# A diffusion block with windowed attention and 64 routed experts: batch 6's routing steps, the sends of rows, the expert accumulators and the last sums rearranged

## Chip, core and metric

The kernel runs on one core of one Trainium2 chip. The metric is the device time of one execution in microseconds. Of the kernel before three runs were made: 907.73, 908.15 and 908.41 us, median 908.15.

## What is computed

Input x is 8 batches of 512 tokens with 256 features, all fp32. In short:

```
mod = silu(c) @ wmod                     # 6 rows of 256 per batch: sa, ca, ga, sb, cb, gb
h = layernorm(x) * (1 + ca) + sa
x = x + ga * attention(h)                # 16 heads of 16, keys within 64 tokens, out projection
h = layernorm(x) * (1 + cb) + sb
scores = sigmoid(h @ gate_w.T)           # 64 experts in 8 groups
# best 4 groups by the sum of their two best (scores + bias), best 8 experts in them
# weights = scores of these, divided by their sum, times 2.5
# each expert takes its first 256 tokens (in token order), at most
y = (silu(buf @ w_gate[e]) * (buf @ w_up[e])) @ w_down[e]   # 256 -> 128 -> 256, per expert
x = x + gb * (sum over a token's experts of weight * y)
```

## The kernel before

It is written engine by engine, each with an instruction stream of its own and semaphores between them; nothing is scheduled by a compiler. There are three stages.

**Attention, with routing behind it.** The loop `batches` goes over the 8 batches. One batch has 20 slots (`SLOTS`: 4 groups of 4 heads, 5 key tiles each; slot = 5g + u). In each slot TensorE computes transposed scores for two pairs of heads (`scoresT`), ScalarE takes their exponentials (`exps`, semaphore `exp`, two per slot) and TensorE multiplies them by the values (`values`, semaphore `pv`, two per slot, but issued in bunches: key tiles 0 to 2 of a group at u = 3, tiles 3 and 4 at the next group's u = 0). VectorE takes row maxima ahead (L1453). Hidden between these lie the steps of the next batch (projections; tables `AT`, `SECOND`) and those of the batch before: output projection, x1, second layer norm, router. When each of these comes is written out by hand in the tables `BEHIND_IT` (batches up to 4), `LAST_BUT_TWO` (batch 5) and `LAST_BUT_ONE` (batch 6), which give slots of the batch that follows. Batch 7 has no batch behind it, its steps (`late_...`) come in halves of 256 tokens when attention is over.

The steps of a batch b that matter here, in order: `c_stats` (VectorE), `c_rstd` (GpSimd, four tiny operations per half of the tokens, L723 to L729, the last makes `nmean`), `c_xhat` (ScalarE, normalises into the row buffer H, L918, waits for `nmean`), `c_norm` (VectorE, L1508), `c_h2T` and `c_lg` (TensorE; they wait for both halves), `c_ex` (ScalarE, L929), `c_route` in 12 parts (VectorE, L1638; part 9 makes the chosen-expert mask and running counts, part 11 writes the weights and the token number into H, L1708 and L1710), `e_cnt` (TensorE, counts of tokens ahead), `e_key` (VectorE; makes `dest`, the slot numbers, L1724). For batch 7, `late_route` and `late_key` do the same per half (L1555, L1613, L1629).

**Sends.** GpSimd then writes each token's row to its 8 experts' buffers in DRAM (`slots_d`) by indirect DMAs (`send`, L746), one per 128 tokens and choice: 32 per batch. In the loop they are spread over slots: `SENDS_OF[b]` says how many in which slot, counted from the start of the following batch (slot 18 to 19, then 20 and on in the batch after that). The first send of a slot waits for `exp` of the slot before, the others for `pv`. GpSimd works in program order, and within a slot `a_rstd`, `wrap` and `c_rstd` stand ahead of the sends. What doesn't fit, and batch 7's 32, is sent behind attention, with the two halves of `c_rstd` of batch 7 between (L811 to L820).

**Experts.** When all sends have landed, SP loads the 256 rows of an expert (`load_slots`, 12 buffers `xg`, up to 8 experts ahead; from 12 on it waits for the rows of expert e - 12 to be added, L636), TensorE turns them (L1382), multiplies (L1394), ScalarE and VectorE make silu times up, TensorE multiplies by w_down (L1404), ScalarE scales with the token's weight (`scale_y`, L1018, 6 buffers `ys`), and GpSimd adds the rows to the tokens' sums in DRAM by two indirect DMAs per expert (`scatter`, L832; L827 writes without adding for the first expert of an accumulator). There are three accumulators `acc_d`; `ACC[e]` says which expert uses which, and a scatter waits until the last expert on the same accumulator has landed. Expert weights have 36 buffers and are loaded up to 36 experts ahead.

**Last sums.** SP loads the third accumulator into `f2` (`load_f2`, 512 KB per batch in four DMAs) and the gate row into `fg` (1 MB) behind the expert loop's other loads; then, when all rows are added, the other two accumulators of each batch into `fa` (L662). VectorE makes three sums per batch of 128x1024 (L1861, L1863, L1865: first plus second accumulator, plus the third, times the gate; the residual x1 is in accumulator 0 already and divided by the gate), and SP stores each (L666).

```
            def send_some(bt, rows, now, slot):
                for n, i in enumerate(rows):
                    if n == 0:
                        after(pool, "exp", now, 2 * slot)
                    else:
                        after(pool, "pv", now, 2 * slot)
                    send(bt, i)
```

## Time and profile before

| | |
|---|---|
| Runs | 907.73, 908.15, 908.41 us |
| The profiled execution | 907.57 us, span in the profile 905.8 us |
| TensorE busy | 681.8 us (75%) |
| GpSimd busy | 509.8 us (56%) |
| VectorE busy | 478.9 us (53%) |
| ScalarE busy | 394.4 us (44%) |
| Mean DMA rate | 211 GB/s, 191.47 MB |

The profiled execution's own time lies 1.8 us over its span (what is around the program) and 0.6 us under the median. In the timeline, attention runs to about 525 us, the sends behind it to 613, the experts to 868, the last sums to the end. Engines are called PE (TensorE), DVE (VectorE), ACT (ScalarE), POOL (GpSimd) and SP (the queue of most DMAs) in the rows. L with a number is a line of the kernel before. A busy share is a mean over stages with different limits, so the stages are read one by one. In a timeline the bracket at the end of a row is the idle time of the engine ahead of it and what ended it; "issue" there is time in which the engine waited for nothing that the profile shows.

### The profile page before, as it was taken

The page shows a single profiled execution, that of the slowest core. Times are in us where ns is not written, and L with a number is a line of the kernel's source. Part 1 is how long each engine was busy: PE and PEld are TensorE (multiplying, and loading weights), DVE is VectorE, ACT ScalarE, POOL GpSimd, SP SyncE. Part 2 cuts the span into 40 slices and gives each one's busy share as a digit, 9 for nine tenths or more (in the row PEclk, how much of TensorE's full clock was granted, in tenths as well). Part 3 has the DMA queues.
Part 4 walks back from the last instruction along what each step waited for, and adds up shares of the span by engine and source line. Part 5 has one row for each costly group of instructions (what it writes and reads, how often), then busy time and mean ns, then how long its engine had stood idle before and what let it go on. Part 6 is the DMA issues. An engine that isn't in the chain of part 4 may idle for free.

```text
span 905.8 us, 15461 instructions
## 1 busy us (share of the span) xinstructions
PE 681.8 (75%) x4760; PEld 466.9 (52%) x4787; DVE 478.9 (53%) x1964; ACT 394.4 (44%) x876; POOL 509.8 (56%) x519
## 2 busy tenths in 40 slices
PE   5679899999999999999797942006999888888000
PEld 3335556556566565565455522005888777676000
DVE  3065559869698697786787736201222222222048
ACT  2336566657566566665644511002444333334000
POOL 4000002057577476575767767772788888888810
PEclk9869999999999999999989975557999999999555
DMA  8684896748757577373536794107999998898997
GB/s 325 164 339 164 276 354 211 245 139 271 266 172 259 175 257 254 117 237 123 191 120 182 210 292 120 28 4 224 274 288 266 266 175 160 162 159 160 204 307 318
DMA packets 168334, 191.47 MB, mean 211 GB/s; under 512 B 22137, under 2 KB 150677, under 8 KB 168252
## 3 DMA queue, kind: packets, MB, share of 16 engines
q1 hardware_dynamic: 132220, 134.15, 46.6%
q0 software_dynamic: 30336, 38.03, 20.1%
q10 hardware_dynamic: 5696, 18.30, 5.3%
q8 instruction: 39, 0.64, 0.3%
q14 instruction: 43, 0.35, 0.1%
HBM read 100.64 MB, written 110.67 MB: 233 GB/s over the span
## 4 chain that ended last, share of the span: by engine, by line
PE 47%; POOL 14%; DMA 11%; DVE 10%; issue 9%; ACT 6%; ACTq 1%; SPq 1%; POOLq 0%; DVEq 0%
POOL acc_d L832 8%; PE outT L1171 7%; DMA acc_d<-ys,xg 7%; POOL slots_d L746 5%; PE scoresT L1394 5%; PE scoresT L1151 4%; PE stageA L1092 4%; PE scores L1129 4%; PE scoresT L1155 4%; PE stageA L1110 3%; PE stageC L1212 3%; ACT PT L890 2%; DMA Qs<-MT 2%; DVE junk L1453 2%; PE turns L1181 2%
## 5 line engine op out<-in xcount | busy, mean ns | idle before, releaser
L746 POOL DMA_INDIRECT slots_d<-H,dest x256 | 260.8, 1019 | 155.2 <-issue 87.9
L832 POOL DMA_INDIRECT acc_d<-ys,xg x124 | 191.6, 1545 | 55.0 <-issue 29.2
L1453 DVE CUSTOM_DVE_ANT_0 junk<-scores,mask 128x256 bf16<-128x256 f32 (+1 forms) x512 | 170.9, 387 | 72.1 <-PE scores L1129 70.8
L890 ACT ACTIVATE PT<-scoresT 128x512 f32<-128x512 f32 (+1 forms) x320 | 150.5, 509 | 47.5 <-PE scoresT L1155 45.6
L1394 PE MATMUL scoresT<-xgT,wgu 128*128 128x256 f32 x512 | 125.5, 388 | 17.5 <-ACT xgT L1005 17.4
L1151 PE MATMUL scoresT<-mask,identb 128*128 128x512 bf16 (+1 forms) x320 | 110.3, 345 | 18.7 <-ACT PT L890 14.5
L1394 PEld LDWEIGHTS scoresT<-xgT,wgu 128*128 128x128 f32 x512 | 95.4, 192 | 40.8 <-ACT xgT L1005 27.9
L1155 PE MATMUL scoresT<-Qs,Ks 98*128 98x256 bf16 (+1 forms) x640 | 110.9, 255 | 0.0
L1129 PE MATMUL scores<-Ks,Qs 96*128 96x256 bf16 (+1 forms) x512 | 93.7, 266 | 4.0 <-DVE mrowmax L1453 1.8
L1155 PEld LDWEIGHTS scoresT<-Qs,Ks 98*128 98x128 bf16 x640 | 64.0, 100 | 38.2 <-issue 8.6
L1171 PE MATMUL outT<-PT,Va 128*32 128x256 f32 (+1 forms) x1280 | 80.4, 356 | 1.8
L1842 DVE COPY xgT<-stageA 128x256 f32<-128x256 f32 x32 | 13.6, 425 | 118.2 <-PE stageA L1382 118.2
L874 ACT ACTIVATE parts<-stageA,bqk 128x512 bf16<-128x512 f32 x78 | 53.6, 687 | 42.3 <-PE stageA L1092 37.3
L1382 PE MATMUL scores<-ident,xg 128*128 128x128 f32 x128 | 24.9, 277 | 47.2 <-DMA xg<-slots_d 47.2
L1842 DVE COPY xgT<-stageC 128x256 f32<-128x256 f32 x32 | 13.6, 425 | 75.6 <-PE stageC L1382 75.6
L1151 PEld LDWEIGHTS scoresT<-mask,identb 128*128 128x128 bf16 x320 | 31.8, 99 | 39.8 <-ACT PT L890 22.2
L1005 ACT ACTIVATE xgT<-scores 128x256 f32<-128x256 f32 x64 | 24.7, 386 | 62.5 <-PE scores L1382 62.5
L1129 PEld LDWEIGHTS scores<-Ks,Qs 96*128 96x128 bf16 x512 | 44.4, 99 | 13.1 <-DVE mrowmax L1453 7.0
L1092 PE MATMUL stageA<-hT,wqkv 128*128 128x512 f32 x104 | 50.2, 605 | 0.0
L1171 PEld LDWEIGHTS outT<-PT,Va 128*32 128x32 f32 (+1 forms) x1280 | 28.9, 109 | 40.9 <-issue 25.2
L1018 ACT ACTIVATE ys<-outT,xg 128x256 f32<-128x256 f32 x64 | 26.9, 471 | 52.4 <-DMA acc_d<-ys,xg 45.3
L1018 ACT ACTIVATE ys<-turns,xg 128x256 f32<-128x256 f32 x64 | 26.9, 471 | 50.8 <-DMA acc_d<-ys,xg 43.1
(260 smaller groups left out, 1059.9 us busy)
## 6 DMA issues: line engine op xcount, KB each, us to landing
xg<-slots_d SPq DMA_DIRECT2D x64, 324.0 KB, 4.0
slots_d<-blank ACTq DMA_DIRECT2D x26, 648.0 KB, 5.2
parts_d<-parts SPq DMA_DIRECT2D x32, 384.0 KB, 3.4
Qs<-parts_d SPq DMA_DIRECT2D x96, 128.0 KB
Ks<-parts_d SPq DMA_DIRECT2D x90, 128.0 KB
acc_d<-zero SPq DMA_DIRECT2D x32, 272.0 KB
wgu<-L_ffn_w_gate_dram SPq DMA_DIRECT2D x64, 128.0 KB, 3.6
wgu<-L_ffn_w_up_dram SPq DMA_DIRECT2D x64, 128.0 KB, 3.7
```

What stands on the lines that cost most here:

```text
L746: pool.indirect_dma_start(out=slots_d[:, :], in_=H2[bt.par][:, t, :], in_offset=None, out_offset=bass.IndirectOffsetOnAxis(ap=dest[bt.par] ...
L832: pool.indirect_dma_start(out=acc_d[ACC[e]][:, :], in_=ys[e % NY][:, h, :], in_offset=None, out_offset=bass.IndirectOffsetOnAxis(ap=xg[e % ...
L874: sc_.activation(parts[:, j, k, :], bank[:, :], ACT.Identity, scale=SCALE if f < 2 else 1.0, bias=bqk[:, f:f + 1]).then_inc(sems["part"], 1)
L890: sc_.activation(PT[m % NPT][:, :, 0:w], src, ACT.Exp).then_inc(sems["exp"], 1)
L1018: sc_.activation(ys[e % NY][:, h, :], yb[:, h * D:(h + 1) * D], ACT.Copy, scale=xg[e % NX][:, h, D + e:D + e + 1]).then_inc(mo["yc"], 1)
L1092: last = mm(bank[:, :], wqkv[:, k, f * P:(f + 1) * P], hT[:, k, BAND:BAND + S], start=(k == 0), stop=(k == C - 1))
L1129: last = mm(bS[n % 2][:, i * 2 * P + lo:i * 2 * P + hi], q[0:MROW, h, t * P:(t + 1) * P], kk[0:MROW, h, t * P + lo:t * P + hi], start=True ...
L1151: mm(bST[m % 2][:, 0:2 * (hi - lo)].rearrange("p (h q) -> p h q", h=2), identb[:], half.unsqueeze(1).to_broadcast([P, 2, hi - lo]), start= ...
L1155: last = mm(bST[m % 2][:, i * (hi - lo):(i + 1) * (hi - lo)], kk[0:KROWS, h, u * P:(u + 1) * P], q[0:KROWS, h, lo:hi], start=False, stop=T ...
L1171: last = mm(bO[32 * j:32 * j + 32, lo:hi], Va[bt.par][rows, tile_of(u), HQ * g + j, :], PT[m % NPT][rows, i, 0:hi - lo], start=(u == 0), s ...
L1394: last = mm(bST[par][:, a * CAP:(a + 1) * CAP], wgu[e % NW][:, a, k, :], xgT[par][:, k, :], start=(k == 0), stop=(k == C - 1))
L1453: ins = v.tensor_tensor_reduce(out=junk[:, i, lo:hi], in0=bS[n % 2][:, i * 2 * P + lo:i * 2 * P + hi], in1=mask[:, lo:hi], scale=1.0, scal ...
```

## The change

- For batch 6 (`LAST_BUT_ONE`) `c_rstd`'s second half, `c_xhat`, `c_norm` and the first `c_h2T` come a slot later; the routing parts come up to two slots earlier, the count at slot 17 instead of 19.
- Batch 5's rows are sent three per slot instead of two, batch 6's four in slots 18 and 19 instead of two, and behind attention 11 and 2 sends instead of 8 and 2 stand around the halves of `c_rstd`. In every batch the second and later sends of a slot wait for `exp` (this slot's first) instead of `pv`.
- The third accumulator is used up to expert 26 instead of 53. Its loads into `f2` (32 DMAs of 128 KB) and that of `fg` go into the expert loop of SP, one per expert from 27 on, each behind a wait for TensorE's output of that expert. For that half of `f2` lies below the expert buffers in SBUF and half above.
- ScalarE scales expert 0 right behind taking expert 1's rows.
- GpSimd makes the last sums of batches 1 and 4, with a semaphore of its own; VectorE those of the other six. SP stores in order of the batches as before.

```diff
--- before.py
+++ after.py
@@ -113,13 +113,13 @@
     x1_store=(11,),
     xs=(10,),
     stats2=(4, 5),
-    c_rstd=(5, 5),
-    xhat=(5, 6),
-    norm2=(6, 7),
-    h2T=(8, 10),
+    c_rstd=(5, 6),
+    xhat=(6, 7),
+    norm2=(7, 8),
+    h2T=(9, 10),
     lg=(11,),
-    route=(11, 12, 13, 13, 13, 14, 14, 15, 15, 16, 17, 18),
-    cnt=(19,),
+    route=(11, 12, 12, 13, 13, 13, 14, 14, 15, 15, 16, 16),
+    cnt=(17,),
     key=(17,),
 )
 
@@ -199,8 +199,8 @@
 SENDS = sends_from(22, (1, 2, 2, 2, 1, 2, 1, 2, 2, 1, 2, 2, 2, 1, 2, 1, 2, 2, 1, 1))
 SENDS_OF = [SENDS] * B
 SENDS_OF[B - 4] = sends_from(22, (2, 2, 2, 2, 2, 2, 2, 2, 2, 2, 2, 2, 2, 2, 2, 2))
-SENDS_OF[B - 3] = sends_from(18, (2, 2, 2, 2, 2, 2, 2, 2, 2, 2, 2, 2, 2, 2, 2, 2))
-SENDS_OF[B - 2] = sends_from(18, (2, 2, 28))
+SENDS_OF[B - 3] = sends_from(18, (3, 3, 3, 3, 3, 3, 3, 3, 3, 3, 2))
+SENDS_OF[B - 2] = sends_from(18, (4, 4, 24))
 SENDS_OF[B - 1] = {}
 
 
@@ -417,10 +417,12 @@
         end = ExitStack()
         sb = lambda name, shape, dt=F32: sbt(end, name, shape, dt)
         fg = sb("fg", [P, B, D])
-        sb("beyond_the_start", [P, 7656 - B * D])
+        f2 = [sb(f"f2_{i}", [P, T, D]) for i in range(B // 2)]
+        sb("beyond_the_start", [P, 7656 - B * D - B // 2 * T * D])
         NF = 8
-        f2 = [sb(f"f2_{i}", [P, T, D]) for i in range(B)]
         fa = [sb(f"fa{i}", [P, 2, T, D]) for i in range(NF)]
+        sb("beside_experts", [P, NW * 3 * D - NF * 2 * T * D + NX * 2 * HW + 2 * C * CAP + 4 * CAP + NY * 2 * D])
+        f2 += [sb(f"f2_{i}", [P, T, D]) for i in range(B // 2, B)]
         end.close()
         eng_moe = dict(
             w_ld=[sem(f"weights_loaded{i}") for i in range(NW)],
@@ -430,12 +432,14 @@
             sg=sem("silu_done"),
             hm=sem("hidden_done"), yp=sem("expert_out_made"), yc=sem("expert_out_scaled"),
             f2_ld=sem("third_sums_loaded"),
-            f_ld=[sem(f"sums_loaded{i}") for i in range(NF)], fsum=sem("last_sums"),
+            f_ld=[sem(f"sums_loaded{i}") for i in range(NF)], fsum=sem("last_sums"), psum=sem("last_sums_by_gpsimd"),
             f_st=sem("out_stored"),
         )
         mo = eng_moe
 
-        ACC = [e % 3 if e < 54 else e % 2 for e in range(E)]
+        THIRD_ENDS = 27
+        POOL_SUMS = (1, 4)
+        ACC = [e % 3 if e < THIRD_ENDS else e % 2 for e in range(E)]
         NCONST = 26
         NSET = 4
         BLANKS = 32
@@ -625,11 +629,10 @@
             load_c(last)
             rows = slots_d.rearrange("(h p e) c -> p h e c", h=2, p=P)
 
-            def load_f2(b):
-                rows_added(sp, max(e for e in range(E) if ACC[e] == 2) + b)
-                for t in range(T):
-                    sp.dma_start(f2[b][:, t, :], acc_d[2][b * S:(b + 1) * S, :].rearrange("(p t) d -> p t d", p=P)[:, t, :]
-                                 ).then_inc(mo["f2_ld"], 16)
+            def load_f2(b, t):
+                rows_added(sp, max(e for e in range(E) if ACC[e] == 2))
+                sp.dma_start(f2[b][:, t, :], acc_d[2][b * S:(b + 1) * S, :].rearrange("(p t) d -> p t d", p=P)[:, t, :]
+                             ).then_inc(mo["f2_ld"], 16)
 
             def load_slots(e):
                 if e >= NX:
@@ -650,10 +653,12 @@
                 if e + NW < E:
                     sp.wait_ge(mo["yp"], e + 1)
                     load_w(slice(e + NW, e + NW + 1), e)
-
-            for b in range(B):
-                load_f2(b)
-            sp.dma_start(fg[:], mod_d[:, 4, :].unsqueeze(0).to_broadcast([P, B, D])).then_inc(s_fg, 16)
+                if THIRD_ENDS <= e < THIRD_ENDS + B * T:
+                    sp.wait_ge(mo["yp"], e + 1)
+                    load_f2(*divmod(e - THIRD_ENDS, T))
+                if e == THIRD_ENDS + B * T:
+                    sp.wait_ge(mo["yp"], e + 1)
+                    sp.dma_start(fg[:], mod_d[:, 4, :].unsqueeze(0).to_broadcast([P, B, D])).then_inc(s_fg, 16)
             for e in range(E - NY, E):
                 rows_added(sp, e)
 
@@ -666,15 +671,10 @@
                 sp.dma_start(out[i].rearrange("o (p t) d -> p (o t) d", p=P), fa[n][:, 0]).then_inc(mo["f_st"], 16)
 
             for b in range(B):
-                if b >= NF:
-                    sp.wait_ge(mo["f_st"], 16 * (b - NF + 1))
-                load_f(slice(b, b + 1), b % NF)
-                if b >= NF - 1:
-                    sp.wait_ge(mo["fsum"], 3 * (b - NF + 2))
-                    store_f(slice(b - NF + 1, b - NF + 2), (b + 1) % NF)
-            for b in range(B - NF + 1, B):
-                sp.wait_ge(mo["fsum"], 3 * (b + 1))
-                store_f(slice(b, b + 1), b % NF)
+                load_f(slice(b, b + 1), b)
+            for b in range(B):
+                sp.wait_ge(mo["psum" if b in POOL_SUMS else "fsum"], 3 * sum((i in POOL_SUMS) == (b in POOL_SUMS) for i in range(b + 1)))
+                store_f(slice(b, b + 1), b)
             sp.wait_ge(mo["f_st"], 16 * B)
 
 
@@ -751,10 +751,7 @@
             def send_some(bt, rows, now, slot):
 
                 for n, i in enumerate(rows):
-                    if n == 0:
-                        after(pool, "exp", now, 2 * slot)
-                    else:
-                        after(pool, "pv", now, 2 * slot)
+                    after(pool, "exp", now, 2 * slot + min(n, 1))
                     send(bt, i)
 
             def body(prev, now, nxt):
@@ -808,13 +805,13 @@
                 for i in range(sum(n for s, n in SENDS_OF[bt.b].items() if s < 2 * SLOTS), T * K):
                     send(bt, i)
             sent_before = sum(n for s, n in SENDS_OF[B - 2].items() if s < SLOTS)
-            for i in range(sent_before, sent_before + 8):
+            for i in range(sent_before, sent_before + 11):
                 send(pre, i)
             c_rstd(last, 0)
-            for i in range(sent_before + 8, sent_before + 10):
+            for i in range(sent_before + 11, sent_before + 13):
                 send(pre, i)
             c_rstd(last, 1)
-            for i in range(sent_before + 10, T * K):
+            for i in range(sent_before + 13, T * K):
                 send(pre, i)
             for i in range(T * K):
                 send(last, i)
@@ -841,6 +838,18 @@
                 if same:
                     rows_added(pool, same[-1])
                 scatter(e)
+
+            pool.wait_ge(s_fg, 16)
+            pool.wait_ge(mo["f2_ld"], 16 * B * T)
+            for n, b in enumerate(POOL_SUMS):
+                pool.wait_ge(mo["f_ld"][b], 32)
+                a = fa[b]
+                gp.tensor_tensor(a[:, 0], a[:, 0], a[:, 1], ALU.add).then_inc(mo["psum"], 1)
+                pool.wait_ge(mo["psum"], 3 * n + 1)
+                gp.tensor_tensor(a[:, 0], a[:, 0], f2[b][:], ALU.add).then_inc(mo["psum"], 1)
+                pool.wait_ge(mo["psum"], 3 * n + 2)
+                gp.tensor_tensor(a[:, 0], a[:, 0], fg[:, b, :].unsqueeze(1).to_broadcast([P, T, D]), ALU.mult
+                                 ).then_inc(mo["psum"], 1)
 
 
         @block.scalar
@@ -1023,7 +1032,9 @@
                 silu(e)
                 if e < E - 1:
                     take_x(e + 1)
-                if e > 0:
+                if e == 0:
+                    scale_y(0)
+                if e > 1:
                     scale_y(e - 1)
             scale_y(E - 1)
 
@@ -1855,15 +1866,19 @@
 
             dve.wait_ge(s_fg, 16)
             dve.wait_ge(mo["f2_ld"], 16 * B * T)
+            n = 0
             for b in range(B):
-                a = fa[b % NF]
-                dve.wait_ge(mo["f_ld"][b % NF], 32 * (b // NF + 1))
+                if b in POOL_SUMS:
+                    continue
+                dve.wait_ge(mo["f_ld"][b], 32)
+                a = fa[b]
                 v.tensor_tensor(a[:, 0], a[:, 0], a[:, 1], ALU.add).then_inc(mo["fsum"], 1)
-                dve.wait_ge(mo["fsum"], 3 * b + 1)
+                dve.wait_ge(mo["fsum"], n + 1)
                 v.tensor_tensor(a[:, 0], a[:, 0], f2[b][:], ALU.add).then_inc(mo["fsum"], 1)
-                dve.wait_ge(mo["fsum"], 3 * b + 2)
+                dve.wait_ge(mo["fsum"], n + 2)
                 v.tensor_tensor(a[:, 0], a[:, 0], fg[:, b, :].unsqueeze(1).to_broadcast([P, T, D]), ALU.mult
                                 ).then_inc(mo["fsum"], 1)
+                n += 3
 
 
 _INS = ["L0_attn_x", "L0_attn_w_qkv", "L0_attn_b_qkv", "L0_attn_w_out", "L0_attn_b_out", "L0_ffn_gate_w",
```

## Rows read from the trace of the kernel before

**Rows 1.** GpSimd's timeline behind attention: start us, us, engine line op out<-in [idle before <-releaser].
```profile
525.70 0.97 POOL L746 DMA_INDIRECT slots_d<-H,dest  x1 [6.16 <-DVE H L1710]
...
541.13 0.22 POOL L723 TENSOR_SCALAR ve<-mv 128x2 f32<-128x2 f32 x1
...
570.99 1.69 POOL L746 DMA_INDIRECT slots_d<-H,dest  x1 [0.30 <-DVE dest L1629]
...
611.35 0.97 POOL L746 DMA_INDIRECT slots_d<-H,dest  x1 [0.31 <-issue]
```

**Rows 2.** GpSimd's timeline at the end of the experts.
```profile
848.88 1.54 POOL L832 DMA_INDIRECT acc_d<-ys,xg  x1 [0.57 <-DMA acc_d<-ys,xg]
...
857.02 1.54 POOL L832 DMA_INDIRECT acc_d<-ys,xg  x1 [1.04 <-DMA acc_d<-ys,xg]
...
862.56 1.54 POOL L832 DMA_INDIRECT acc_d<-ys,xg  x1 [0.30 <-issue]
```

**Rows 3.** VectorE's timeline in the tail, first and last of 24 sums.
```profile
873.41 1.23 DVE L1861 TENSOR_TENSOR fa<-fa 128x1024 f32<-128x1024 f32 x1 [35.16 <-DMA fa<-acc_d]
...
901.50 1.22 DVE L1865 TENSOR_TENSOR fa<-fa,fg 128x1024 f32<-128x1024 f32 x1
```

**Rows 4.** Stretch 885 to 890: stretch, us, PE, PEld, DVE, ACT, POOL busy, PEclk, DMA share, GB/s.
```profile
885.00:890.00 5.00, 0.00 (x0) 0.00 (x0) 4.90 (x5) 0.00 (x0) 0.00 (x0) 0.50 1.02 406
```

**Rows 5.** ScalarE's timeline in batch 7.
```profile
492.69 1.09 ACT L918 ACTIVATE H<-x,nmean,rs 128x256 f32<-128x256 f32 x2 [4.61 <-POOL nmean L729]
...
502.82 0.75 ACT L890 ACTIVATE PT<-scoresT 128x256 f32<-128x256 f32 x2
...
509.83 0.38 ACT L929 ACTIVATE ex<-stageC 128x256 f32<-128x256 f32 x1 [1.33 <-PE stageC L1230]
```

**Rows 6.** GpSimd's timeline in batches 6 and 7.
```profile
473.06 0.98 POOL L746 DMA_INDIRECT slots_d<-H,dest  x1 [0.30 <-ACT PT L890]
...
489.69 0.97 POOL L746 DMA_INDIRECT slots_d<-H,dest  x1 [0.30 <-issue]
...
490.73 0.45 POOL L723 TENSOR_SCALAR ve<-mv 128x2 f32<-128x2 f32 x1
...
492.38 0.20 POOL L729 TENSOR_TENSOR nmean<-nmean,rs 128x2 f32<-128x2 f32 x1
```

**Rows 7.** VectorE's timeline, batches 6 and 7.
```profile
468.23 0.18 DVE L1724 TENSOR_SCALAR dest<-near 128x32 uint32<-128x32 f32 x1
...
524.60 0.16 DVE L1710 COPY H<-token 128x4 int32<-128x4 int32 x1
...
560.97 0.17 DVE L1629 TENSOR_SCALAR dest<-near 128x16 uint32<-128x16 f32 x1
```

**Rows 8.** GpSimd's timeline at the start of the experts.
```profile
628.06 1.58 POOL L832 DMA_INDIRECT acc_d<-ys,xg  x1 [15.74 <-ACT ys L1018]
...
637.80 1.55 POOL L832 DMA_INDIRECT acc_d<-ys,xg  x1 [1.08 <-ACT ys L1018]
```

**Rows 9.** Scatter-adds issued from 728 to 750: issue to landing.
```profile
DMA to landing us min/median/max: 3.7/4.1/5.3
```

**Rows 10.** Stretch 740 to 760, columns as in rows 4.
```profile
740.00:760.00 20.00, 17.68 (x91) 14.25 (x89) 4.48 (x11) 7.53 (x21) 16.65 (x12) 1.00 0.92 160
```

**Rows 11.** Chain that ended last: start us, us, what.
```profile
862.56 5.71 DMA acc_d<-ys,xg
```

**Rows 12.** GpSimd's timeline in the setup.
```profile
2.26 0.56 POOL L698 TENSOR_SCALAR minus<-ident 128x128 bf16<-128x128 f32 x1
...
13.68 0.90 POOL L795 MEMSET Va<- 128x960 f32 x1
...
17.15 0.29 POOL L717 COPY hT<-hT 128x128 f32<-128x128 f32 x1
```

**Rows 13.** One sum of VectorE and one send of GpSimd, timelines of both.
```profile
505.72 1.22 DVE L1514 TENSOR_TENSOR x<-x,mr 128x1024 f32<-128x1024 f32 x1
...
506.10 1.69 POOL L746 DMA_INDIRECT slots_d<-H,dest  x1 [0.30 <-issue]
```

## The prediction

> **What bounds the kernel now.** The page's costliest groups come first: GpSimd's indirect sends of rows (L746) and its scatter-adds (L832) head them. The timelines by engine then show three stretches that GpSimd or VectorE sets. (a) After attention GpSimd issues the 64 sends of batches 6 and 7 without a pause, the first at 525.70, the last at 611.35, one each 1.28 us; the first had waited 6.16 us for VectorE's routing of batch 6 [rows 1]. The experts can't begin before the last has landed. (b) In the experts GpSimd issues two scatters per expert, 1.85 us apart, so 3.69 us per expert [rows 2]. TensorE, faster, waits. (c) In the last 37 us VectorE makes 24 sums back to back, 873.41 to 902.72, 29.3 us, three per batch of 3.66 [rows 3], while the DMAs run at 410 GB/s at full share [rows 4].
>
> The attention stretch before (a) counts as far as it sets when batch 6 is routed. Batch 7's attention has one large stall: ScalarE stands 4.61 us at the normalised rows of batch 6 until 492.69, released by GpSimd's `nmean`, whose c_rstd began at 490.73 right behind a send [rows 5, 6]. So c_rstd was late because of GpSimd's queue: 14 sends of batch 5, 473.06 to 489.69, each at 1.28 with no wait between [rows 6].
>
> **Part 1: three sends per slot, weaker waits.** Under two per slot GpSimd issues 7x2 = 14 sends of batch 5 ahead of c_rstd(6, first half), from slot 18 to slot 4. With three it issues 21. The new waits (`exp` for `pv`) take away GpSimd's idle time before 470, and batch 4's sends are done a few us sooner; but batch 5's still wait for its `dest`, made at 468.23 [rows 7]. From `H` at 524.60+0.16 to the first send at 525.70 passed 0.94 [rows 1, 7], so the first of batch 5 goes at about 469.3. 21x1.28 = 26.9 puts c_rstd's first half at 496.2 instead of 490.73: **5.5 us later**. Three more sends (3.84) and c_rstd's own 1.85 (490.73 to 492.58 [rows 6]) put the second half at 502.1 to 503.9. In other bodies c_rstd waits for VectorE or for nothing long, and I cost the new waits there at nothing: TensorE covers them.
>
> **Part 2: rows a slot further.** Shifting `c_rstd`, `xhat`, `norm2` by a slot lets ScalarE do slot 6's exponentials at about 491 ahead of the wait. Then it waits for `nmean` until 498.1; slot 7's exponentials; then it waits again, until 503.9, for the second half; slot 8's at 505 to 506. TensorE, two score banks deep, stands with it. Before, slot 9's exponentials ran at 502.82 and `ex` at 509.83 [rows 5], 7.0 us later; now slot 9 is at 506.6, so `ex` comes at 513.6 to 514.4. **+4.2 us.** Bounds: 0 (the stop only moves, and later slots take it up) and +6 (`h2T` of slot 9 takes TensorE some 1 us, and more of such small delays).
>
> **Part 3: routing two parts per slot, the count at slot 17.** From `ex` on VectorE runs without an idle time worth naming to `H` at 524.60 [rows 7], so moving its parts to earlier slots brings nothing: it works them off at its own pace. The count isn't the last wait either (`key` starts when VectorE is free). What changes: `norm_o` (0.7 us) now stands behind the histogram instead of ahead of it, and TensorE stands some 3 us at slot 17 for it; that delays batch 7's own end, which has 10 us of slack (below). Zero. So the first send of batch 6 goes at 525.70+4.2.
>
> **Part 4: behind attention.** 64 sends stay 64: slots 18 and 19 hold 8 instead of 4, then 11, 2 and the rest. c_rstd of batch 7 comes behind 19 sends instead of 12, so 4.2+7x1.28 = 13.2 us later than 541.13 [rows 1]. Batch 7's first `dest` follows: 560.97 [rows 7] goes to 574.2, and its first send, 570.99 before [rows 1], is wanted at 575.2. It just arrives; its second half has some 10 us. Zero here, but there is no slack left, and up to 1 us could show. Sum of parts 1 to 4: **+4.2**.
>
> **Part 5: first scale_y earlier.** Expert 0's scatters began at 628.06 [rows 8]. ScalarE can now scale it right behind `take_x(1)`, some 2.2 us earlier. But GpSimd waits again at expert 3, whose first scatter goes at 637.80, released by ScalarE, which was released by TensorE [rows 8]. That doesn't move. Zero.
>
> **Part 6: third accumulator ends at expert 27; f2 and fg loaded between experts.** In 27 to 53 an expert waits for the rows of the last but one, not the last but two. A scatter lands 4.1 us (median) after its issue there, 5.3 at most [rows 9]; the next on the same accumulator starts 3x1.85 = 5.54 after it, and GpSimd starts about 0.3 after a landing. So up to 5.24 costs nothing. The SP queue now adds a 128 KB load per expert behind the 324 KB of slots, where the DMAs are 0.92 busy in 740 to 760 [rows 10]. From 848 on, with such loads in bursts, two waits came, of 0.57 and 1.04 where 0.30 is usual [rows 2]: 1.0 us in some 8 experts. At that rate 33 experts cost 4.1; without any effect 0. I take 2: only the slower half of landings crosses 5.24, and a wait gives the next expert room. Against it: those two waits go (-1.0), and the last scatter, 862.56, no longer lands beside the 1 MB of fg; it took 5.7 us [rows 11] and will take 4.7 (-1.0). SP's first f2 load waits for expert 26's rows, so the slots of experts 36 on come 3 experts (11 us) later; 12 slot buffers and TensorE's lead over GpSimd cover it. Uncovered it would be 4 us of landing, once. Sum **0**, bounds -2 and +2.5.
>
> **Part 7: two of eight batches summed by GpSimd.** VectorE keeps 18 sums: 6x3.66 = 22.0 us. GpSimd gets 6 of 128x1024 with two operands in SBUF. No row has such a one. Below: it sets 960 columns in 0.90 [rows 12], so 0.96. Above: a scaled copy of 128 columns takes 0.56 [rows 12] against 0.20 for an operation on two columns [rows 6], so 1024 take 3.1. Between: its plain copy of 128 columns takes 0.29 [rows 12], 0.7 to 1 ns per column over its start, and with two operands to read twice that, **2.1 us**, which I take. 6x2.1 = 12.6.
>
> Do they run side by side? The rows say no, in one direction: a GpSimd send issued during a VectorE sum of two SBUF operands ends 0.84 us behind that sum. The sum 505.72+1.22 = 506.94, the send 506.10+1.69 = 507.79 [rows 13]; the same at 570.99 [rows 1] against 570.62+1.22. A free send takes 0.97. So GpSimd can't read while VectorE sums, and what one does adds to the other: 22.0+12.6 = 34.6 against 29.3, **+5.3 us** (bounds by the price: 27.8, -1.5; 40.6, +11.3). If they did run beside each other, VectorE would end at 897.5, held by the loads (8.4 MB at 0.41 are in at about 891.7), and the 12.6 MB of the stretch would end it near 901.5: **-4.3**.
>
> The Trainium skill, SBUF — State Buffer, "Who interferes with whom", says more than the row: a VectorE instruction with two SBUF inputs and a GpSimd instruction that reads SBUF exclude each other, whichever comes first. By it a GpSimd sum also stops VectorE's; the sum stays +5.3. The skill's GPSIMD Engine Reference, "3.1 Elementwise", gives 4497 ns for a GpSimd sum of 2048 fp32 columns, so by its figure some 2.25 us for 1024, and the tail's sum would be 22.0+13.5, +6.2. No row of this profile shows either.
>
> **Sum.** 4.2+0+0+5.3 = +9.5 on the profiled execution's 907.57 (span 905.8) is 917.1. The median of the runs is 0.58 above that execution: **917.7**.
>
> **The rivals.**
> Side by side: GpSimd's and VectorE's sums overlap after all (for it: only GpSimd was seen to wait, and its port time may be a small part of its instruction). Tail -4.3, the rest +4.2: 908.0, in a band of 904 to 911. It ends faster than before as soon as parts 1 to 6 cost less than 2.4 us. 0.24.
> Side by side, and the stall doesn't reach the routing (0 for parts 1 to 4): 903.9. This is the one on the other side: the place is the tail, the price 4.3, and it decides when the last batch's stop stays under 2.4 us. For it speaks that TensorE has slack at slots 12 to 19; against it that `ex` hangs on the second c_rstd by a chain with no slack. 0.12.
> Turns are taken in the tail, but the stall doesn't reach: 913.5. 0.16.
> My forecast, both: 917.7, own range 913.5 to 922. 0.48.
>
> **Numbers.** A measurement tells 0.2% (1.8 us) from nothing here. Faster: 0.12, and half of the first rival, 0.12: 0.24. Same: 0.12. Slower: the rest, 0.64. The range takes in the side-by-side cases and most of the upper bound: 903.5 to 922.
>
> **What would show it.** Right: ScalarE waiting on `nmean` twice in batch 7, some 6 and 4 us; batch 6's c_rstd at 496; the first send of batch 6 near 530, 64 without a pause behind it; sums in the tail stretched or spaced by 2 us, ending near 909 plus the shift. Wrong: c_rstd(6) at or before 491; `ex` before 511; VectorE's 18 sums at 1.22 with no gap beside GpSimd's; scatters spaced over 1.9 us on average (part 6 too low).

## The result, and where the time went

The changed kernel takes **922.35 us** (median of 4 runs, 917.35 to 924.2) where the one before, in the same session, takes 908.28 us (907.73 to 909.94): ratio **1.0155**, 95% interval 1.0126 to 1.0183. Forecast were 917.7 us and a range to 922.0; the direction is right, the size 4.65 us short, and the result lies 0.35 us above the range. The profiled execution took 924.2 us (span 922.4 us) against 907.57 us (905.8 us), 16.6 us more. It is read at six points, each the same instruction in both traces:

| point | before | after | later by | gained since the last |
|---|---|---|---|---|
| exponentials of slot 5, batch 7 | 485.85 | 487.72 | 1.87 | 1.87 |
| `ex` of batch 7 | 509.83 | 516.07 | 6.24 | 4.37 |
| last send | 611.35 | 617.68 | 6.33 | 0.09 |
| first scatter-add of expert 3 | 637.80 | 646.31 | 8.51 | 2.18 |
| first last sum on VectorE | 873.41 | 885.02 | 11.61 | 3.10 |
| end of VectorE's last sum | 902.72 | 919.39 | 16.67 | 5.06 |

The rows that answer to those of before. ScalarE's timeline of the changed kernel, batch 7 (as rows 5):

```profile
499.46 1.09 ACT L927 ACTIVATE H<-x,nmean,rs 128x256 f32<-128x256 f32 x2 [5.85 <-POOL nmean L729]
...
505.21 1.09 ACT L927 ACTIVATE H<-x,nmean,rs 128x256 f32<-128x256 f32 x2 [3.54 <-POOL nmean L729]
...
516.07 0.39 ACT L938 ACTIVATE ex<-stageC 128x256 f32<-128x256 f32 x1 [1.33 <-PE stageC L1241]
```

The one wait of 4.61 us for `nmean` has become two, 5.85 and 3.54 us. GpSimd's timeline of the changed kernel (as rows 6, 1, 8 and 2, then the last sums, which no row of before has):

```profile
470.79 0.97 POOL L746 DMA_INDIRECT slots_d<-H,dest  x1 [1.06 <-ACT PT L899]
...
496.68 0.97 POOL L746 DMA_INDIRECT slots_d<-H,dest  x1 [0.30 <-issue]
...
497.72 0.23 POOL L723 TENSOR_SCALAR ve<-mv 128x2 f32<-128x2 f32 x1
...
503.47 0.23 POOL L723 TENSOR_SCALAR ve<-mv 128x2 f32<-128x2 f32 x1
...
532.16 0.97 POOL L746 DMA_INDIRECT slots_d<-H,dest  x1 [15.68 <-DVE dest L1735]
...
617.68 0.98 POOL L746 DMA_INDIRECT slots_d<-H,dest  x1 [0.30 <-issue]
...
633.49 1.58 POOL L829 DMA_INDIRECT acc_d<-ys,xg  x1 [14.84 <-ACT ys L1027]
...
639.77 1.01 POOL L824 DMA_INDIRECT acc_d<-ys,xg  x1 [2.81 <-ACT ys L1027]
...
646.31 1.55 POOL L829 DMA_INDIRECT acc_d<-ys,xg  x1 [1.26 <-ACT ys L1027]
...
848.20 1.55 POOL L829 DMA_INDIRECT acc_d<-ys,xg  x1 [2.92 <-DMA acc_d<-ys,xg]
...
876.03 1.55 POOL L829 DMA_INDIRECT acc_d<-ys,xg  x1 [0.30 <-issue]
...
888.34 2.62 POOL L847 TENSOR_TENSOR fa<-fa 128x1024 f32<-128x1024 f32 x1 [10.75 <-DMA fa<-acc_d]
891.04 3.20 POOL L849 TENSOR_TENSOR fa<-fa,f 128x1024 f32<-128x1024 f32 x1
...
904.16 3.20 POOL L851 TENSOR_TENSOR fa<-fa,fg 128x1024 f32<-128x1024 f32 x1
```

c_rstd of batch 6 starts at 497.72 instead of 490.73, right behind a send. GpSimd had waited longer ahead of its sends of batch 6 (15.68 us for `dest`, since batch 5's were out earlier), so the time won there went into a wait. The 64 sends then took 85.5 us from the first to the last start, as before (85.65): no gap opened. In the experts GpSimd now waits for landed rows. All scatter-adds issued from 728 to 750, issue to landing, changed kernel (as rows 9):

```profile
DMA to landing us min/median/max: 3.9/5.3/6.7
```

That is a short window of 12. Over the whole stretch in question, the 54 scatter-adds of experts 27 to 53, first the kernel before, then the changed one:

```profile
DMA to landing us min/median/max: 3.7/4.0/5.3
...
DMA to landing us min/median/max: 3.8/4.8/6.7
```

The stretch from the first scatter-add of expert 27 to that of expert 53, in the kernel before:

```profile
726.57:822.71 96.14, 84.38 (x420) 68.00 (x418) 21.71 (x53) 36.93 (x106) 80.30 (x52) 1.00 0.90 162
```

Stretches of the changed kernel (columns as rows 4; the second is that of experts 27 to 53):

```profile
620.00:640.00 20.00, 15.06 (x54) 11.88 (x55) 2.69 (x7) 5.43 (x12) 3.40 (x3) 0.66 0.78 232
...
735.39:834.42 99.03, 83.39 (x420) 68.30 (x418) 21.33 (x53) 36.55 (x103) 80.64 (x52) 1.00 0.96 197
905.00:910.00 5.00, 0.00 (x0) 0.00 (x0) 4.93 (x4) 0.00 (x0) 2.36 (x1) 0.50 0.37 150
```

Over experts 27 to 53 the DMAs move 197 GB/s at a share of 0.96 where they moved 162 at 0.90, a scatter-add lands in 4.8 us (median) instead of 4.0, and the stretch takes 99.03 us instead of 96.13. In the 20 us from 740 to 760 alone the rate is 241 against 160 [rows 10]; the first loads of `f2`, issued in a bunch from 737.64 on, fall there. From 905 on the DMAs are at 0.37: in the tail they wait for the engines, where before they ran at 406 GB/s [rows 4]. VectorE's timeline in the tail of the changed kernel (as rows 3):

```profile
885.02 1.23 DVE L1875 TENSOR_TENSOR fa<-fa 128x1024 f32<-128x1024 f32 x1 [31.48 <-DMA fa<-acc_d]
...
890.75 1.28 DVE L1875 TENSOR_TENSOR fa<-fa 128x1024 f32<-128x1024 f32 x1 [1.99 <-DMA fa<-acc_d]
892.08 3.25 DVE L1877 TENSOR_TENSOR fa<-fa,f 128x1024 f32<-128x1024 f32 x1
...
905.19 3.24 DVE L1879 TENSOR_TENSOR fa<-fa,fg 128x1024 f32<-128x1024 f32 x1
...
918.17 1.22 DVE L1879 TENSOR_TENSOR fa<-fa,fg 128x1024 f32<-128x1024 f32 x1
```

Five of VectorE's sums take 3.24 to 3.35 us instead of 1.22, each beside a sum of GpSimd of 3.20; when GpSimd is done they are back at 1.22.

### The profile page after: what moved, and what is told of

The parts are those of the page before. It is cut to its first block, busy times and chain, and to the rows that moved or that the text cites. A ratio compares the mean times of both kernels' runs of the same rounds, so it can differ in the third digit from the quotient of the medians.

```text
span 922.4 us, 15494 instructions
## 1 busy us (share of the span) xinstructions
PE 689.8 (75%) x4760; PEld 471.5 (51%) x4787; DVE 482.7 (52%) x1958; ACT 396.0 (43%) x876; POOL 529.1 (57%) x525
## 4 chain that ended last, share of the span: by engine, by line
PE 46%; POOL 17%; issue 11%; DVE 11%; DMA 7%; ACT 5%; SPq 1%; ACTq 1%; DVEq 0%; POOLq 0%
POOL acc_d L829 10%; PE outT L1182 7%; POOL slots_d L746 5%; PE stageA L1103 5%; PE scoresT L1162 4%; PE scoresT L1405 4%; PE scores L1140 4%; PE scoresT L1166 4%; DMA acc_d<-ys,xg 3%; PE stageA L1121 3%; PE stageC L1223 3%; ACT PT L899 2%; DVE junk L1464 2%; PE turns L1192 1%; PE stageC L1241 1%
## 5 line engine op out<-in xcount | busy, mean ns | idle before, releaser
L1405 PE MATMUL scoresT<-xgT,wgu 128*128 128x256 f32 x512 | 127.4, 393 | 23.3 <-ACT xgT L1014 23.3
L1405 PEld LDWEIGHTS scoresT<-xgT,wgu 128*128 128x128 f32 x512 | 97.3, 195 | 46.3 <-ACT xgT L1014 32.3
L1182 PE MATMUL outT<-PT,Va 128*32 128x256 f32 (+1 forms) x1280 | 82.5, 364 | 1.8
```

Of the source, the lines that this page charges most:

```text
L1182: last = mm(bO[32 * j:32 * j + 32, lo:hi], Va[bt.par][rows, tile_of(u), HQ * g + j, :], PT[m % NPT][rows, i, 0:hi - lo], start=(u == 0), s ...
L1405: last = mm(bST[par][:, a * CAP:(a + 1) * CAP], wgu[e % NW][:, a, k, :], xgT[par][:, k, :], start=(k == 0), stop=(k == C - 1))
```

## The experiments

All but four ran in sessions where the kernel before takes 907.4 to 908.2 us. The other four (e9 to e12) ran in one where it takes 985.75; what that session shows is told at the end. Each ratio is against runs of before in the same session. Where an edit is a part of the change, its hunks are those shown in the change. No kernel leaves any part of the computation out.

**e1_sums: part 7 alone.**

```diff
+        POOL_SUMS = (1, 4)
...
+            for n, b in enumerate(POOL_SUMS):
...
```

VectorE's loop goes over the other six batches.

> The kernel before, with part 7 alone: GpSimd makes the last sums of batches 1 and 4. Theory (they take turns at the SBUF read port): as forecast +5.3 us, VectorE's sums stretched from 1.22 to about 3.25 us while GpSimd has work (the 2.0 over are what GpSimd holds the port). Rival (side by side): -4.3 us, VectorE's 18 sums at 1.22. Second rival: in the changed kernel the stretching comes from something else of the change (the place of f2 in SBUF); then this run is faster or equal.

Measured 913.28 us (911.89 to 917.26), ratio 1.0072 (1.0044 to 1.0099). VectorE's timeline in its tail, first sum and one beside GpSimd:

```profile
874.01 1.22 DVE L1872 TENSOR_TENSOR fa<-fa 128x1024 f32<-128x1024 f32 x1 [35.44 <-DMA fa<-acc_d]
...
884.34 3.25 DVE L1876 TENSOR_TENSOR fa<-fa,fg 128x1024 f32<-128x1024 f32 x1
...
907.16 1.22 DVE L1876 TENSOR_TENSOR fa<-fa,fg 128x1024 f32<-128x1024 f32 x1
```

From first start to last end 34.37 us (908.38-874.01), the same as in the whole change, against 29.3: the price is this part's own and needs none of the others. Both side-by-side rivals fall.

**e2_attn: parts 1 to 4 alone.** Edit: the slot table, both lists of sends, the waits in `send_some`, and 11, 2 for 8, 2 behind attention.

> The kernel before, with parts 1 to 4 alone (slots of batch 6, two routing parts per slot, three sends per slot, new waits, 4+4+11+2 sends). Theory (c_rstd of batch 6 comes late behind 21 sends): +4.2 us as forecast, +4.6 by the trace of the changed kernel; ScalarE waits for nmean twice in batch 7, about 6 and 3.5 us. Rival (the 6.5 us by which the sends of batch 6 came late were mostly the 1.9 us already lost before plus noise of the chip): under +2 us.

Measured 911.83 us (909.4 to 916.76), ratio 1.0061 (1.0039 to 1.0083). ScalarE's timeline, batch 7:

```profile
497.36 1.09 ACT L915 ACTIVATE H<-x,nmean,rs 128x256 f32<-128x256 f32 x2 [5.83 <-POOL nmean L729]
...
503.09 1.09 ACT L915 ACTIVATE H<-x,nmean,rs 128x256 f32<-128x256 f32 x2 [3.53 <-POOL nmean L729]
...
514.11 0.38 ACT L926 ACTIVATE ex<-stageC 128x256 f32<-128x256 f32 x1 [1.33 <-PE stageC L1227]
```

`ex` is 4.28 us later than before [rows 5] and the last send 3.4 (614.76). These four parts make this cost without the other three; e9_send5 and e13_send5 below narrow it to one list of sends.

**e3_experts: part 6 alone.** Edit: `THIRD_ENDS = 27`, the memory of `f2`, and the loads of `f2` and `fg` in SP's loop over the experts.

> The kernel before, with part 6 alone (third accumulator up to expert 26, f2 and fg loaded between the experts). By my forecast 0 (-2 to +2.5). By the trace of the changed kernel +3.1: waits on the last but one expert's rows in some 14 places (2.6 us over the usual), one of 2.9 us behind the 1 MB load of fg, less 1.0 for the waits of before and less 1.9 for the last landing. Rival (the waits come from the later start of the experts or from parts 1 to 4): 0 or faster.

Measured 910.54 us (907.67 to 911.87), ratio 1.0029 (1.0014 to 1.0044). GpSimd waits in 16 places for landed rows, 10.8 us with the usual 0.30 in each. Landing of its scatter-adds of experts 27 to 53, and one such wait:

```profile
DMA to landing us min/median/max: 3.6/5.1/6.8
```
```profile
735.75 1.54 POOL L836 DMA_INDIRECT acc_d<-ys,xg  x1 [1.15 <-DMA acc_d<-ys,xg]
```

From the first scatter-add of expert 27 to that of expert 53 it takes 100.26 us where before takes 96.13. So part 6 isn't free. Whether the two accumulators or the loads do it, the next two tell.

**e4_scale: part 5 alone.** Edit: `scale_y(0)` behind `take_x(1)`.

> The kernel before, with part 5 alone (ScalarE scales expert 0 earlier). Theory: 0, since expert 3's first scatter is released by TensorE's pace; first scatter 2.2 us earlier, expert 3's where it was. Rival (it delays silu(1) or changes when TensorE's clock rises, and so explains the 2.2 us that the experts' start lost in the changed kernel): +2 us, with the granted clock still 0.5 for some 10 us behind the experts' first product.

Measured 907.78 us (905.64 to 909.96), ratio 1.0003 (0.9987 to 1.0019). GpSimd's timeline at the start of the experts:

```profile
626.71 1.58 POOL L832 DMA_INDIRECT acc_d<-ys,xg  x1 [13.23 <-ACT ys L1018]
...
632.18 1.02 POOL L827 DMA_INDIRECT acc_d<-ys,xg  x1 [2.00 <-ACT ys L1018]
...
638.72 1.55 POOL L832 DMA_INDIRECT acc_d<-ys,xg  x1 [1.26 <-ACT ys L1018]
```

The first scatter comes 2.5 us sooner behind the last send (14.20 us instead of 16.71), and waits of 2.00, 0.71 and 1.26 us at the following experts take it all back: expert 3 starts 26.2 us behind the last send, 26.45 before.

**e5_third: two accumulators from expert 27 on, the code of the loads left as it was.** The loads move all the same: each batch's waited for the rows of an expert from 53 on, and now only for one from 26 on. They go out in one bunch behind SP's other loads, all 32 from 822.17 to 838.71, where before they took from 828.40 to 858.51.

```diff
-        ACC = [e % 3 if e < 54 else e % 2 for e in range(E)]
+        ACC = [e % 3 if e < 27 else e % 2 for e in range(E)]
```

> The kernel before, with the third accumulator ending at expert 26 and the loads of f2 and fg left where they were. Theory (the waits come from the loads that now stand between the experts): within 0.5 us of before, a wait of GpSimd for rows of the last but one expert here and there by 0.1 us. Rival (two accumulators alone are too few at this pace): +2 us, waits in most experts from 27 on.

Measured 909.28 us (906.87 to 912.84), ratio 1.0014 (0.9999 to 1.0029). Its scatter-adds of experts 27 to 53, and a wait behind that stretch:

```profile
DMA to landing us min/median/max: 3.8/4.1/5.9
...
835.30 1.54 POOL L832 DMA_INDIRECT acc_d<-ys,xg  x1 [1.43 <-DMA acc_d<-ys,xg]
```

The medians lie between theory and rival and decide nothing; the interval also meets that of e3_experts. The traces do. In all twelve with three accumulators that far, experts 27 to 53 take 96.1 to 96.5 us; here they take 96.50, with landings as before; in the five with the loads between (the change, e3, e6, e12, e14) 99.0 to 100.4. So two accumulators cost next to nothing there by themselves. Behind expert 53 this run loses 2.3 us (42.14 from there to the last scatter-add, 39.85 before), with five waits beside the bunch of loads, and it gains 2.0 at the last landing. The loads lengthen the landings; the two accumulators make the lengthened landings count. For the 1 MB of the gate e16_best shows the other side: with three accumulators it is loaded at 764.3 and the stretch takes 96.14.

**e6_fgend: e3_experts with the gate's load (`fg`, 1 MB) back behind the experts.**

> The kernel of e3_experts with the 1 MB load of fg put back behind the expert loop (as in the kernel before, after expert 60's rows); the 32 loads of f2 stay between the experts. Theory (fg costs one long wait between experts and gives 1.9 us back at the last landing, so its move is worth -0.7 in all at most): about as slow as e3_experts, +1.6 to +2.6 over before, no wait over 1.5 us. Rival (fg is the cost of part 6): 0 or below.

Measured 911.62 us (909.75 to 913.67), ratio 1.0028 (1.0012 to 1.0044), the same as e3_experts; the rival falls. GpSimd's timeline shows where the load's price went:

```profile
867.33 1.54 POOL L835 DMA_INDIRECT acc_d<-ys,xg  x1 [3.20 <-DMA acc_d<-ys,xg]
```

The 1 MB holds up the scatter-adds in flight where it meets a wait for two accumulators: 2.92 us at 848.20 in the change, 3.20 at 867.33 here. How much varies: in e3_experts, where it goes out at 831.50, the longest wait behind it is 1.35. The expectation that a late place would leave no long wait is wrong.

**e7_rows: e2_attn with the old numbers of sends** (two per slot for batch 5; 2, 2 and then 8, 2 for batch 6); the rows a slot further, the earlier routing parts and the weaker waits are kept.

> The kernel before with the new waits (exp for pv) and the new slots of batch 6, but two sends per slot and 2, 8 and 2 as before. Theory (only the seven more sends ahead of c_rstd made the changed kernel slow; without them the new waits let batch 5's sends begin 3 us earlier): c_rstd's first half at about 489 instead of 490.7, first send of batch 6 at 524 or before, -1.5 us. Rival (the shift of the slots itself costs, as the rows of expert h2T come later): +1 us or more.

Measured **904.69 us** (902.18 to 906.53), ratio **0.9959** (0.9935 to 0.9983), faster. ScalarE's timeline, batch 7:

```profile
491.72 1.08 ACT L915 ACTIVATE H<-x,nmean,rs 128x256 f32<-128x256 f32 x2
...
495.92 1.09 ACT L915 ACTIVATE H<-x,nmean,rs 128x256 f32<-128x256 f32 x2 [0.80 <-ACT MT L892]
...
505.24 0.39 ACT L926 ACTIVATE ex<-stageC 128x256 f32<-128x256 f32 x1 [1.33 <-PE stageC L1227]
```

c_rstd of batch 6 comes at 488.43, ScalarE waits for no `nmean` there, and `ex` is 4.6 us earlier than before. The new slots and the weaker waits together are a gain of 3.7 us by the ratio, where 1.5 was expected: the wait of 4.61 us [rows 5] is gone. Which of them brings how much was not tested apart; c_rstd starts 2.3 us earlier than before, and the rows are wanted a slot later. The third send per slot takes the gain, and more than as much again.

**e8_pe: all last sums by TensorE** (three products with the identity per half batch, gathered in PSUM; VectorE multiplies by the gate from PSUM).

```diff
+                    for k, src in enumerate((fa[b][:, 0], fa[b][:, 1], f2[b])):
+                        last = mm(bank[:, :], ident[:], src[:, 2 * i:2 * i + 2, :].rearrange("p t d -> p (t d)"), start=(k == 0),
+                                  stop=(k == 2))
...
-                v.tensor_tensor(a[:, 0], a[:, 0], a[:, 1], ALU.add).then_inc(mo["fsum"], 1)
...
```

> The kernel before, but the last sums of all batches are made by TensorE (three products with the identity per half batch, added up in PSUM), VectorE only multiplies by the gate (16 operations on 128x512 of about 0.69 us). Theory (the tail is set by VectorE's 29.3 us, with the transfers 4.3 us behind it as the next limit): -4 us, transfers at full share until the stores are out. Rival (TensorE at its lower clock needs 5 us per batch and becomes the bound): 0 or slower, +10 us.

Measured 923.32 us (922.49 to 924.82), ratio 1.0166 (1.0142 to 1.0189), 15.1 us slower: TensorE is the bound, as in the rival, but not at the rival's lower clock (5.2 us per batch came at full clock). Stretch 880 to 900, and VectorE's timeline:

```profile
880.00:900.00 20.00, 20.00 (x48) 8.80 (x47) 5.13 (x8) 0.00 (x0) 0.00 (x0) 1.00 0.82 332
```
```profile
884.25 0.69 DVE L1872 TENSOR_TENSOR fa<-scoresT,fg 128x512 f32<-128x512 f32 x1 [1.88 <-PE scoresT L1426]
...
886.83 0.69 DVE L1872 TENSOR_TENSOR fa<-scoresT,fg 128x512 f32<-128x512 f32 x1 [1.89 <-PE scoresT L1426]
```

TensorE is busy throughout, with its clock granted in full (1.00), and a half batch still takes it 2.58 us (886.83-884.25), so 0.86 us for one product of 512 fp32 columns; VectorE waits 1.9 us for each. The Trainium skill, FP8 and Floating Point Precision, "TensorE Precision Notes", says that a true fp32 product takes four passes through the array. By it an estimate for 512 columns, at one column a cycle of 2.4 GHz, is 4x512/2.4, or 0.853 us, which the trace agrees with.

**e9_send5 and e13_send5: e7_rows with batch 5's sends at three per slot**, batch 6's as before. (The routing parts are those of e7_rows, in the new slots, and not "as before".)

> e7_rows (rows a slot further, routing parts as before, two sends per slot) with only batch 5's sends set to three per slot; batch 6's stay at 2, 2 and then 8 and 2 behind attention. Theory A (five to seven more sends ahead of c_rstd(6) are the price): ScalarE waits again twice for nmean, about 5.8 and 3.5 us, ex near 514, and the kernel comes back to about 1.005 to 1.006 of before (912 to 913 us). Rival (the sends of batch 6, four per slot and eleven behind attention, are the price): no wait on nmean, 0.996 (904.5 us).

> The kernel of e9_send5 again, on whichever chip: with before near 908 us, theory A (batch 5's sends are the price) says ScalarE waits about 5.8 and 3.5 us for nmean of batch 7, ex near 514, 1.005 to 1.006 of before (912 to 913 us). Rival: no wait on nmean, 0.996 (904.5 us).

e13 measured 912.36 us (911.13 to 915.21), ratio 1.0055 (1.0034 to 1.0075). ScalarE's timeline, batch 7:

```profile
498.05 1.09 ACT L915 ACTIVATE H<-x,nmean,rs 128x256 f32<-128x256 f32 x2 [7.35 <-POOL nmean L729]
...
503.79 1.09 ACT L915 ACTIVATE H<-x,nmean,rs 128x256 f32<-128x256 f32 x2 [3.54 <-POOL nmean L729]
```

`ex` comes at 514.33. The whole price of parts 1 to 4 (1.0061) stands in this one list; what was done to batch 6's sends costs nothing that can be told. e9 gave 1000.37 us (998.4 to 1004.95), ratio 1.0129 (1.0091 to 1.0168), in the session where before takes 985.75. There ScalarE didn't wait for `nmean` in batch 7 (attention itself was slower, and GpSimd's queue in time), so its price is another one. Part of it shows in GpSimd's queue: the 64 sends take 93.3 us instead of 85.3, with a wait of 4.11 us at 689.03 for batch 7's `dest`. Why `dest` is late there stays open.

**e10_mix and e15_mix: before, with the last sums of batches 2 and 5 by TensorE** as in e8_pe, taken by VectorE in the order 0, 1, 3, 4, 2, 6, 7, 5.

> Before with the last sums of batches 2 and 5 made by TensorE (three products with the identity per half batch, 2.57 us each half by e8_pe, beside VectorE's other sums) and VectorE's gate product read from PSUM (0.69 us a half). VectorE then needs 6 x 3.66 + 4 x 0.69 = 24.7 us instead of 29.3. Theory: nothing shares a port and TensorE is done in time, so about -4 us (904 us). Rival: the transfers are the bound (12.7 MB at 412 GB/s is 30.8 us from the first load on), so at most -2 us.

> The kernel of e10_mix again. There VectorE's sums took 24.7 us from first to last end instead of 29.3, and the kernel ended 4.3 us behind them instead of 3.1: 3.4 us shorter, which the noise of that chip hid (0.9982, 0.9947 to 1.0017). Here -3.4 us: 904.8 us, 0.9963. Rival: the transfers are the bound, -2 us or less.

e10: 986.09 us (977.46 to 994.8), ratio 0.9982 (0.9947 to 1.0017), nothing to tell. e15: 904.62 us (902.3 to 906.16), ratio **0.9966** (0.9951 to 0.9981). VectorE's timeline of e15 in the tail:

```profile
874.04 1.23 DVE L1879 TENSOR_TENSOR fa<-fa 128x1024 f32<-128x1024 f32 x1 [36.76 <-DMA fa<-acc_d]
...
889.25 1.28 DVE L1874 TENSOR_TENSOR fa<-scores,fg 128x512 f32<-128x512 f32 x2
...
897.75 1.28 DVE L1874 TENSOR_TENSOR fa<-scoresT,fg 128x512 f32<-128x512 f32 x2
```

From first start to last end 25.0 us instead of 29.3, no operation of VectorE stretched, and no wait for TensorE. The share given to GpSimd stretched VectorE's sums (e1_sums), the share given to TensorE left them at 1.21 to 1.23 us. Giving work away pays when the other engine doesn't hold up the giver and is done in time.

**e11_best and e16_best: e7_rows, e15_mix, and the gate's load at expert 40,** while three accumulators are still in use:

```diff
+                if e == 40:
+                    sp.dma_start(fg[:], mod_d[:, 4, :].unsqueeze(0).to_broadcast([P, B, D])).then_inc(s_fg, 16)
```

> e7_rows and e10_mix together, and the gate load of 1 MB moved from behind the experts to expert 40. Sum of the parts if they add up: 0.9959 of before (-3.7), -4 for the sums (or -2 by the rival), and at most -2 for the load ahead of the last landing: about 899 us; 902 if the rival holds and the load gives nothing.

> The kernel of e11_best again: e7_rows (0.9959, -3.7), the sums of e15_mix (-3.4) and the gate load at expert 40 (up to -2): 0.990 to 0.992, 899 to 901 us. If the parts don't add up, 904.

e11: 982.24 us (972.99 to 986.4), ratio 0.9954 (0.9922 to 0.9987). e16: **898.69 us** (895.72 to 899.96), ratio **0.9892** (0.9871 to 0.9912), which beats both kernels; 899 to 901 was expected if the parts add up. The gate's load cost nothing at expert 40 (the only wait for landed rows is one of 1.02 us at expert 60), and the first sum came 8.95 us behind the last scatter instead of 10.85.

**e12_again and e14_again: the change itself.**

> The change itself once more, for a second trace. Theory: 1.0155 of before (922 us) with the same two waits on nmean, the same sums near 3.2 us, the same waits of GpSimd on rows landed; the late rise of TensorE's clock at the start of the experts is chance, so expert 3's first scatter-add may come 26.5 us behind the last send (as before) instead of 28.6. Rival: the late rise belongs to the change, and comes back at 28.6.

> The change again. 1.0155 of before (922 us). If the late clock was chance, expert 3's first scatter-add comes 26.2 to 26.7 us behind the last send and the profiled run is about 2 us shorter than 924; if it belongs to the change, 28.6 us.

e12: 1004.53 us (1002.21 to 1012.11), ratio 1.0194 (1.0148 to 1.024). e14: 921.22 us (919.03 to 923.64), ratio 1.015 (1.0127 to 1.0173). GpSimd's timeline of e14:

```profile
616.27 0.98 POOL L746 DMA_INDIRECT slots_d<-H,dest  x1 [0.30 <-issue]
...
643.10 1.55 POOL L829 DMA_INDIRECT acc_d<-ys,xg  x1 [1.26 <-ACT ys L1027]
...
847.64 1.55 POOL L829 DMA_INDIRECT acc_d<-ys,xg  x1 [3.13 <-DMA acc_d<-ys,xg]
```

Expert 3 comes 26.8 us behind the last send, not 28.6, and 26.7 in e12; e7_rows and e13_send5, without part 5 or 6, show 28.65 and 28.55. The late rise of the clock isn't the change's. But e14 is only 0.5 us shorter in the span (921.9) than the first trace, not 2: its experts took longer (below).

## Why the prediction was right or wrong

The parts alone, by their ratios: 0.61 (parts 1 to 4), 0.03 (part 5), 0.29 (part 6), 0.72 (part 7), in sum 1.65% or 15.0 us; the whole is 1.55% and 1.50% in two sessions. They add up within their intervals, so each step can be judged by itself. The whole is 14.1 us where 9.5 was forecast; of the 4.6 missing, part 6 is 2.6, parts 1 to 4 and part 7 some 1.3 and 1.2, both within their intervals, part 5 0.3, and together they come out 0.9 less than their sum.

**Parts 1 to 4: right** (+4.2; measured +4.37 and +4.28 at `ex`, 5.5 us by the ratio with 3.5 to 7.5). The two waits were forecast at some 6 and 4 us and came at 5.85 and 3.54. c_rstd was forecast 5.5 us later and came 6.99, of which up to 1.87 lay ahead of the part; batch 5's first send was forecast at 469.3 and came at 470.79. That batch 6's sends and the routing parts cost nothing held: no gap in the 64. What the working passed over is that the shifted rows and the weaker waits would have been a gain without the third send; e7_rows shows it.

**Part 5: right,** by the mechanism given: the next waits take it back.

**Part 7: right in the mechanism, and near in the number partly by luck** (+5.3; +5.06 in the change and 5.06 in e1_sums, 6.5 us by the ratio with 4.0 to 9.0). In the pieces of the change's trace: VectorE's own 18 sums of 22.0; five sums held up by 2.03 us each, which is 10.1 (3.25-1.22); and 1.99 for the load of batch 2, in which the first sum of GpSimd passes unnoticed. That is 34.1 of the 34.37. The forecast had six sums held up and no wait for a load; the wait happens to be as long as the sixth. GpSimd's sum was put at 2.1 us, between bounds of 0.96 and 3.1 that came from other operations, and it holds VectorE up for 2.03 to 2.06 (3.28 from one pair to the next, less 1.22). Its first, which met only the end of a VectorE sum at 888.76, was done 2.20 us behind that. The rival's 897.5 for VectorE's end isn't worked out in the prediction; its price doesn't hang on it. VectorE was never seen waiting in the trace of before; the rule in the Trainium skill, SBUF — State Buffer, "Who interferes with whom", that the two exclude each other either way, is what the traces now show in both directions.

**Part 6: the step that failed.** The mechanism was forecast (an expert waits for the rows of the last but one), its size was not. Forecast 0 (+2 for waits, -1.0 for the two old ones, -1.0 for the last landing; bounds -2 and +2.5). Measured 0.29%, 2.6 us (1.3 to 4.0), in e3_experts, and +3.10 between expert 3 and the first sum in the change. By its terms, from the first scatter of expert 3 to the last: 229.7 us instead of 224.8, +5.0 where +1 was put (2.9 over experts 27 to 53, 1.8 behind them, where the wait for the gate row's load stands); from there to the first sum 8.99 instead of 10.85, -1.9 where -1.0 was put. The wrong premise was "a scatter lands 4.1 us (median) after its issue there": that held for a DMA load which the same part raised from 162 to 197 GB/s over experts 27 to 53. Landings there went from 4.0 to 4.8 at the median and from 5.3 to 6.7 at most. So the term of +2 for waits is the one mis-sized: in the change the waits of GpSimd above the usual 0.30 are 5.2 us, 2.6 of it in one wait of 2.92 behind the 1 MB gate row. For that load the working had only the gain at the last landing and no price at its new place, where scatter-adds took up to 7.7 us to land. The upper bound of 4.1 was taken at the rate of rows 2 and was no bound either. The prediction's own sign for a price too low came true: from expert 27 to 53 scatter-adds stand 1.90 us apart (99.03/52) instead of 1.85. e5_third tells the causes apart: with two accumulators and no loads between, that stretch takes 96.50 us and not 99.03 (before: 96.13). The Trainium skill, DMA: Bandwidth & Descriptors, "Latency and other measured facts", gives the latency of an HBM access as 0.2 us on average and 2 at high load; the 0.8 us that the median landing gained has that sign and lies within it, though the traces don't tell memory from queue.

From expert 3 to the first sum seven traces with three accumulators to the end and the loads left behind took 234.2 to 237.0 us (mean 235.8), those of this part (the change, e3, e6, e14) 238.4 to 241.4, e5_third 236.6 and e16_best 233.4. That is also why single traces differ: e14 lost 5.7 us here against before's own trace, the first trace of the change 3.1.

**In no step:** 1.4 us lost near 95 us, ahead of anything the change touches, and 2.18 at the start of the experts. The stretch 620 to 640 of the profiled run has TensorE's granted clock at 0.66 on average; the same stretch of the kernel before:

```profile
620.00:640.00 20.00, 18.59 (x92) 15.72 (x91) 4.53 (x12) 7.66 (x22) 9.03 (x8) 0.95 0.77 230
```

In the change the experts begin 6.4 us later, so part of this is the shift. The rest is the clock. TensorE stood idle behind attention, began the experts at its lower level (1.2 GHz, 616.53 in before and 622.97 in the change), and rose to 2.4 GHz near 622, some 5 us later, in before, and near 633, some 10 us later, in the change. Experts 1 to 3 came later there; that the clock makes all of the 2.18 us is argued, not tested. It comes and goes from trace to trace. These 3.6 us belong to the profiled run; the medians hold a mean of it.

**The rivals.** Side by side (908.0 and 903.9) fell with the first sum of 3.25 us. No stall (913.5) fell with the two waits.

## What to carry over

Ask of every load that is moved into a stretch what it does to the latency of the transfers already there, and set the slack of a wait (here 5.24 us) against the latency under the new traffic, not the old. Take that latency over the whole stretch and not from one short window. A sum of two SBUF operands shared between VectorE and GpSimd brought no gain here, since what one did held up the other; TensorE could take a share, at 0.86 us per product of 512 fp32 columns, as long as it was a small one. An engine's in-order queue is a path of its own: one more send per slot, ahead of a small operation that others wait for, cost 8.7 us (e13_send5 against e7_rows, by the ratios), more than twice the 3.7 that the new slots and weaker waits had brought.

## What the runs showed of the hardware

- A GpSimd sum of 128x1024 fp32 beside a VectorE sum: GpSimd 3.20 us, VectorE 3.25, both again after 3.28. That is 1.22 for VectorE's alone and 2.06 more: what the two take adds up.
- An indirect DMA of GpSimd meets the same limit. Seven sends of the kernel before are issued during a VectorE sum of 128x1024 with two SBUF operands; all seven end 0.84 or 0.85 us behind that sum, and take 1.38 to 1.69 us instead of 0.97.
- In one of the sessions (e9 to e12) before takes 985.75 us (979.15 to 997.71). It is not shown to be another chip: the record gives it the same chip number as the session of e5 to e8, where before takes 908.22. The same kernel, e10_mix there and e15_mix here, has its last send at 693.83 and 611.12, and from there to the end of the span both take 291.8 us: all of it lies ahead of the experts. TensorE's granted clock from 300 to 400 is 0.91 in e10 and 1.00 in e15; that its matmuls there fall from 801 to 656 is more than this explains, and stays open. The experts and the tail kept their times there (in the change VectorE's last sums take 34.38 us in e12, 34.37 in the first trace). Of the gains, e10's can't be told in that spread. e11's is smaller than e16's (0.9954 against 0.9892, and the intervals don't meet), while its experts and tail are as in e16 (233.2 and 24.9 us against 233.4 and 25.1); so what is missing lies ahead of them.
- A scatter-add of rows lands in 3.7 to 5.3 us beside 162 GB/s, and in 3.8 to 6.7 beside 197 (experts 27 to 53); beside the 1 MB load one took 7.7 us in the change and one 8.0 in the kernel before. Its issue on GpSimd stays at 1.54 to 1.55 us in both.
